# Attention scores one head at a time over four PSUM banks, with other bank partners, a later switch of order in the last tiles, and a query projection moved at the first tile

## The chip, the cores and the metric

The kernel runs on one core of one Trainium2 chip. Its time is device microseconds of that core, from the first to the last instruction of one launch. The engines are TensorE (PE, with its weight loads as PEld), VectorE (DVE), ScalarE (ACT), GpSimd (POOL) and SyncE (SP), which issues most transfers.

## What is computed

One block of cross attention and one of a routed feed-forward, both with a residual, on x of 32 batches, 256 positions and 512 features:

```python
def _mha(Q, K, V, Wq, Wk, Wv, Wo, padding_mask, attention_mask):
    n, s, e = Q.shape
    q = (Q @ Wq.T).reshape(n, s, NUM_HEADS, HEAD_DIM).transpose(0, 2, 1, 3)
    k = (K @ Wk.T).reshape(n, s, NUM_HEADS, HEAD_DIM).transpose(0, 2, 1, 3)
    v = (V @ Wv.T).reshape(n, s, NUM_HEADS, HEAD_DIM).transpose(0, 2, 1, 3)
    scores = jnp.einsum('nhqd,nhkd->nhqk', q, k) / math.sqrt(HEAD_DIM)
    scores = jnp.where(pm, scores, neg_inf)
    scores = jnp.where(attention_mask[:, None, :, :], scores, neg_inf)
    attn = jax.nn.softmax(scores, axis=-1)
    attn = jnp.where(jnp.isnan(attn), 0.0, attn)
    out = jnp.einsum('nhqk,nhkd->nhqd', attn, v)
    return out.transpose(0, 2, 1, 3).reshape(n, s, e) @ Wo.T
...
x = x + _mha(_layernorm(x), ctx, ctx, Wq, Wk, Wv, Wo, pad, mask)
x = x + ffn(_layernorm(x))      # one of 8 experts for each position, the same in all batches
```

There are 16 heads of 32 features. Of the 256 keys only the last 64 are not masked in these inputs; the kernel finds that on the chip and takes a short path (`SHORT`), which handles one block of 64 keys (`BK`).

## The kernel before

**Tiling.** The attention works on 64 tiles of 128 queries. Four tiles (two batches) form a group g; q = t mod 4 is a tile's place in its group. For each group PE projects keys (K), transposes them (KT), projects values (V) and queries in four quarters m = 0 to 3 (Q), each a block of twelve matmuls with 512 columns: every product of F32 data is made as three products of rounded high and low parts (`three`). The experts' part follows the attention and isn't touched.

**The four blocks of a tile on PE**, in this order for most tiles (`tiles` in `short_tensor`):
- `transpose_p(t)` (L1609): eight transposes of the normalised weights of tile t into PSUM tensor `pT`; ACT copies them to `pt` in two halves (`pt_copy`, semaphore `p_copied`).
- `project_o(t - 1)`: the output product of the tile before, twelve matmuls.
- `scores(t + 2)` (L1598): the scores of two tiles on. A matmul handles two heads: 64 rows of the query quarter (two heads' features), 128 query columns as weights, and 128 moving columns of `kd`, in which the two heads' keys stand on a diagonal with zeros beside them. Eight such matmuls write 1024 scores a query into `pS[:, 0]`, two banks.
- `weigh_v(t)` (L1622): 16 matmuls of 64 keys by 32 feature columns as weights and 128 queries moving, into `pA`.

After them come the projections of the next groups: two Q blocks where q is 0, one Q where it is 1, V and K where it is 2, KT and a Q where it is 3.

**PSUM.** Eight banks: `pS[:, 0]` (two) for scores, `pS[:, 1]` (two) in turn for all projections and outputs (`bank_of`, `free_bank`, `fills`), `pT` (two), `pA` (two).

**Softmax.** DVE reads the scores from PSUM. For most tiles `bias_scores` adds the mask's bias (L1349, which frees the scores' banks, semaphore `s_drained`) and `shift_biased` finds the maximum and subtracts (L1356, L1360). For the tiles in `pe_masks` (0, 1 and the last five) PE adds the bias itself, with two matmuls of an identity (L1593) ahead of the scores, and `shift_scores` reads PSUM twice (L1330, L1332). ACT makes the exponentials (L1212), DVE sums them (L1366), POOL multiplies by the inverse (`normalise_p`, L1111, semaphore `p_ready`), and PE transposes.

**Order.** Each engine's program is written out by hand. `scores_late(t)` holds for t < 57: scores(t + 2) stands behind project_o(t - 1). `scores_first(t)` holds for t = 57 to 61: scores(t + 2) stands straight behind transpose_p(t), and ACT takes the exponentials earlier in its order. ACT's order in a tile is: copies of the transposes, rounding of new inputs, `ot_high` (L1222, reads `pA`), copies of projections, exponentials of tile t + 2, and y_normalise (L1228) of tile t - 2.

**Keys.** `kt_copy` (ACT) takes the transposed keys from PSUM to `kd` in eight pieces of 32 partitions. `kd` is zeroed once at the start by DVE and POOL (`zeroed`).

The lines around the scores:

```python
for m in range(KC):
    for g2 in range(2):
        half = slice(g2 * 64, (g2 + 1) * 64)
        mm = pe.matmul(pS[:, 0, g2 * 512 + m * P:g2 * 512 + (m + 1) * P],
                       h.qt[half, g % 2, m, q * P:(q + 1) * P], h.kd[half, g % 2, q // 2, m, :],
```

## Time and profile before

| what | value |
|---|---|
| median of 3 runs | 871.42 us (871.19 to 871.42) |
| the profiled execution | 871.33 us, its span 869.5 us |
| PE busy | 97% of the span |
| DVE busy | 80% |
| POOL busy | 72% |
| ACT busy | 50% |

The span runs from the first to the last instruction; 1.8 us of the execution's time lie around it. A PE that is busy all the time isn't at its peak, since matmuls overlap and their ends are modelled; their starts are recorded.
### The profile page before, as it was taken

To read this page: it belongs to the slowest core of one execution; us is meant where nothing else is said; L and a number is where in the kernel's file an instruction comes from. 1 tells how busy PE (TensorE), PEld (TensorE's weight loads), DVE (VectorE), ACT (ScalarE), POOL (GpSimd) and SP (SyncE) were. 2 spreads that over 40 slices of the span, in tenths; PEclk is the share of its full clock that TensorE was granted. 3 is DMA by queue.
4 is the path that set the end of the run, shared out by engine and by line. 5 is a ranking of instruction groups with operands and counts; after the bars stand their busy time and mean duration, and the time that the engine had idled before them with its cause. 6 is when DMAs were issued, how large, how long until landed. Compare 5 with 4: busy or idle time off the path is not lost. (4 is left out here: it accounts for less than half of the span.)

```text
span 869.5 us, 19093 instructions
## 1 busy us (share of the span) xinstructions
PE 843.0 (97%) x6509; PEld 676.7 (78%) x6510; DVE 697.8 (80%) x1021; ACT 434.9 (50%) x762; POOL 630.0 (72%) x826
## 2 busy tenths in 40 slices
PE   8999999999999999999999999999993999999996
PEld 6778887778878888778877888777762788888885
DVE  5988888788888888788888888788778877777774
ACT  5655556565755556555756556555465222222221
POOL 3798778686768668686768668685675677777774
PEclk9999999999999999999999999999996999999998
DMA  9613342524252442524243442522488899999993
GB/s 341 226 43 92 116 136 74 171 74 136 74 157 88 135 135 74 170 77 136 74 154 95 132 133 76 162 83 77 141 270 283 256 282 293 291 281 290 286 293 110
DMA packets 123130, 141.70 MB, mean 163 GB/s; under 512 B 16128, under 2 KB 89376, under 8 KB 120992
## 3 DMA queue, kind: packets, MB, share of 16 engines
q1 hardware_dynamic: 108656, 99.45, 36.5%
q0 software_dynamic: 11360, 35.66, 12.8%
q10 hardware_dynamic: 3024, 5.45, 2.2%
q8 instruction: 49, 0.80, 0.4%
q14 instruction: 41, 0.34, 0.1%
HBM read 90.18 MB, written 51.90 MB: 163 GB/s over the span
## 5 line engine op out<-in xcount | busy, mean ns | idle before, releaser
L1827 PE MATMUL pA<-wf_hl,x_hi 128*128 x560 | 139.2, 391 | 1.8 <-DVE wf_hl L356 1.1
L1827 PEld LDWEIGHTS pA<-wf_hl,x_hi 128*128 128x128 f32 x560 | 105.4, 189 | 24.3 <-issue 2.6
L1111 POOL TENSOR_TENSOR s<-s,row 128x1024 f32<-128x1024 f32 x64 | 121.8, 1903 | 3.1 <-DVE row L1371 3.1
L1768 ACT CAST x_hi<-x2t 128x512 fp32r<-128x512 f32 x70 | 43.5, 621 | 147.1 <-PE pA L1827 136.4
L1519 PE MATMUL pS<-wo_hi,ot_hi 128*128 128x512 f32 x256 | 106.9, 418 | 0.3 <-DVE ot_lo L1375 0.3
L1087 POOL TENSOR_SCALAR y_mom<-y_mom 128x1 f32<-128x1 f32 x64 | 15.9, 248 | 124.9 <-DVE y_mom L1392 123.8
L1519 PE MATMUL pS<-xt_hi,wq_hi 128*128 128x512 f32 x256 | 105.3, 411 | 0.2 <-DVE wq_lo L1412 0.2
L1222 ACT CAST ot_hi<-pA 128x512 fp32r<-128x512 f32 x64 | 37.6, 587 | 128.9 <-PE pA L1622 128.8
L1519 PE MATMUL pS<-wo_lo,ot_hi 128*128 128x512 f32 x256 | 100.9, 394 | 0.0
L1519 PE MATMUL pS<-wo_hi,ot_lo 128*128 128x512 f32 x256 | 100.8, 394 | 0.0
L1519 PE MATMUL pS<-xt_lo,wq_hi 128*128 128x512 f32 x256 | 100.6, 393 | 0.0
L1745 POOL DMA_INDIRECT yg<-y_scratch,gather_rows x70 | 80.1, 1144 | 28.0 <-issue 27.7
L1519 PE MATMUL pS<-xt_hi,wq_lo 128*128 128x512 f32 x256 | 100.2, 391 | 0.0
L1071 POOL TENSOR_TENSOR xt_lo<-xt_raw,xt_hi 128x512 fp32r<-128x512 f32 x64 | 94.4, 1507 | 6.0 <-ACT xt_hi L1179 6.0
L1751 POOL DMA_INDIRECT out_dram<-y,scatter_rows x70 | 72.0, 1029 | 28.1 <-issue 19.8
L1349 DVE TENSOR_TENSOR s<-pS,bias 128x1024 f32<-128x1024 f32 x57 | 69.7, 1223 | 27.8 <-PE pS L1598 27.7
L1791 DVE TENSOR_TENSOR y<-pA,yg 128x512 f32<-128x512 f32 x70 | 48.4, 691 | 48.2 <-PE pA L1827 48.2
L1366 DVE TENSOR_REDUCE row<-s 128x16 f32<-128x1024 f32 x64 | 76.9, 1202 | 11.3 <-ACT s L1212 11.3
L1206 ACT COPY qt<-pS 128x512 f32<-128x512 f32 x64 | 37.6, 587 | 87.0 <-PE pS L1519 87.0
L1598 PEld LDWEIGHTS pS<-kd,qt 64*128 64x128 f32 x1024 | 62.1, 187 | 23.3 <-issue 23.3
L1212 ACT ACTIVATE s<-s,rstd 128x1024 f32<-128x1024 f32 x64 | 73.8, 1153 | 10.1 <-DVE s L1360 9.7
L1360 DVE SCALAR_TENSOR_TENSOR s<-row,s 128x1024 f32<-128x1024 f32 x57 | 76.7, 1346 | 2.0
(134 smaller groups left out, 1937.6 us busy)
## 6 DMA issues: line engine op xcount, KB each, us to landing
xq<-x_scratch SPq DMA_DIRECT2D x280, 64.0 KB
xt_raw<-in_x_t SPq DMA_DIRECT2D x16, 1024.0 KB, 6.9
x<-in_x SPq DMA_DIRECT2D x64, 256.0 KB, 3.2
y_scratch<-y_biased SPq DMA_DIRECT2D x64, 256.0 KB, 2.1
x_scratch<-y_normal SPq DMA_DIRECT2D x64, 256.0 KB, 2.9
wf_hl<-in_wf ACTq DMA_DIRECT2D x5, 1024.0 KB, 6.1
ctx_raw<-in_ctx_t SPq DMA_DIRECT2D x32, 128.0 KB, 3.0
wf_hl<-in_wf SPq DMA_DIRECT2D x3, 1024.0 KB, 8.7
```

The lines of the kernel that those rows point to most:

```text
L1071: pool.tensor_tensor(h.xt_lo[:, k, :], h.xt_raw[:, k, :], h.xt_hi[:, k, :].bitcast(F32), ALU.subtract)\
L1111: pool.tensor_tensor(p, p, h.row[:, t % h.c, 3, :].unsqueeze(2).broadcast_to([P, H, BK]), ALU.mult)\
L1212: act.activation(p, p, ACT.Exp, scale=h.rstd[:, t % h.c, 2:3]).then_inc(exp_ready, 1)
L1349: dve.tensor_tensor(h.s_sb[:, t % h.c, :].rearrange("p (h k) -> p h k", h=H), pS[:, 0, :].rearrange("p (h k) -> p h k", h=H), h.bias[:, t ...
L1360: dve.scalar_tensor_tensor(p, h.row[:, t % h.c, 0, :].unsqueeze(2).broadcast_to([P, H, BK]), FLOOR, p, ALU.max, ALU.subtract).then_inc(shi ...
L1366: dve.tensor_reduce(row[:, 1, :], h.s_sb[:, t % h.c, :].rearrange("p (h k) -> p h k", h=H), AX.X, ALU.add).then_inc(sum_ready, 1)
L1519: mm = pe.matmul(dst, lhs[a], rhs[b], start=(k == 0 and n == 0), stop=(k == KC - 1 and n == 2))
L1598: mm = pe.matmul(pS[:, 0, g2 * 512 + m * P:g2 * 512 + (m + 1) * P], h.qt[half, g % 2, m, q * P:(q + 1) * P], h.kd[half, g % 2, q // 2, m, ...
L1745: pool.indirect_dma_start(yg[:, r, :], None, y_rows, bass.IndirectOffsetOnAxis(ap=gather_rows[:, j:j + 1], axis=0))\
L1751: pool.indirect_dma_start(out, bass.IndirectOffsetOnAxis(ap=scatter_rows[:, j:j + 1], axis=0), y2[:, j % 3, :], None, bounds_check=last_ro ...
L1791: dve.tensor_tensor(y2[:, j % 3, :], pA[:, j % 2, :], yg[:, j % R, :], ALU.add).then_inc(y2_ready, 1)
L1827: return pe.matmul(pA[:, r % 2, :], rows[:, r % 2, c * P:(c + 1) * P], w, start=first, stop=last)
```

## The change

It has four parts.

**Scores.** A matmul now handles one head: 32 rows of features, 64 queries as weights, 64 keys moving. There are 4 (m) x 2 (halves of the queries) x 4 (j, the 32-row quarters) = 32 of them for a tile. Quarter j writes bank 2 + j, 256 columns of it (`pF`). `kd` loses its zeros and half its size, one ACT copy fills it, and the two memsets with their waits are gone. DVE reads and writes the same 1024 elements in patterns with four banks. The heads' order on the host follows. Bias on PE is four matmuls of 256 columns in place of two of 512.

**Banks.** All eight are one tensor `banks`. Projections and outputs take banks 0 and 1, scores 2 to 5, transposes 4 and 5 as before, `pA` 6 and 7. So scores and transposes share two banks: scores(t) waits for `p_copied` of tile t - 2, and transpose_p(t) waits until the scores of tile t + 1 are drained.

**Order in the last tiles.** `scores_first` holds for t = 59 to 61 and `scores_late` for t < 59; PE adds the bias for the last three tiles only. ACT's order follows.

**Tile 0.** project_q(1, 1) stands ahead of scores(2).

```diff
-        self.pe_masks = (0, 1) + tuple(range(self.tiles - 5, self.tiles))
+        self.pe_masks = (0, 1) + tuple(range(self.tiles - 3, self.tiles))
...
     def scores_late(self, t):
-        return t < self.tiles - 7
+        return t < self.tiles - 5
 
     def scores_first(self, t):
-        return self.tiles - 7 <= t < self.tiles - 2
+        return self.tiles - 5 <= t < self.tiles - 2
...
-        pS = top.enter_context(nc.psum_tensor("pS", [P, 2, 2 * 512], F32))
-        pT = top.enter_context(nc.psum_tensor("pT", [P, 2, 512], F32))
-        pA = top.enter_context(nc.psum_tensor("pA", [P, 2, 512], F32))
+        banks = top.enter_context(nc.psum_tensor("banks", [P, 8, 512], F32))
+        pS = banks[:, 0:4, :].rearrange("p (r b) n -> p r (b n)", r=2)
+        pT = banks[:, 4:6, :]
+        pA = banks[:, 6:8, :]
+        pF = banks[:, 2:6, 0:HG * BK].rearrange("p j (m k) -> p j m k", m=KC)
...
             def kt_copy(g):
-                if g == 0:
-                    act.wait_ge(zeroed, 2)
                 act.wait_ge(kt_done, g + 1)
-                for j in range(HG):
-                    r = slice(j * DH, (j + 1) * DH)
-                    src = bank("KT", g)[r, :].rearrange("p (c s k) -> p c s k", c=KC, s=2)
-                    for s in range(2):
-                        ins = act.copy(h.kd[r, g % 2, s, :, (j % 2) * BK:(j % 2 + 1) * BK], src[:, :, s, :])
-                ins.then_inc(kt_copied, 1)
+                act.copy(h.kd[:, g % 2], bank("KT", g).rearrange("p (c s k) -> p s c k", c=KC, s=2)).then_inc(kt_copied, 1)
...
             def scores(t):
                 g, q = divmod(t, h.c)
                 wait(pe, s_drained, t)
+                wait(pe, p_copied, 2 * (t - 1))
...
-                    for g2 in range(2):
-                        pe.matmul(pS[:, 0, g2 * 512:(g2 + 1) * 512].rearrange("p (h k) -> p h k", h=H // 2), ident_r[:],
-                                  h.bias[:, r:r + 1, :].broadcast_to([P, H // 2, BK]), start=True, stop=False)
+                    for j in range(HG):
+                        pe.matmul(pF[:, j], ident_r[:], h.bias[:, r:r + 1, :].broadcast_to([P, KC, BK]), start=True, stop=False)
                 for m in range(KC):
-                    for g2 in range(2):
-                        half = slice(g2 * 64, (g2 + 1) * 64)
-                        mm = pe.matmul(pS[:, 0, g2 * 512 + m * P:g2 * 512 + (m + 1) * P],
-                                       h.qt[half, g % 2, m, q * P:(q + 1) * P], h.kd[half, g % 2, q // 2, m, :],
-                                       start=not biased, stop=not biased or m == KC - 1)
+                    for half in range(2):
+                        rows = slice(half * 64, (half + 1) * 64)
+                        for j in range(HG):
+                            dims = slice(j * DH, (j + 1) * DH)
+                            mm = pe.matmul(pF[rows, j, m, :], h.qt[dims, g % 2, m, q * P + half * 64:q * P + (half + 1) * 64],
+                                           h.kd[dims, g % 2, q // 2, m, :], start=not biased, stop=not biased or m == KC - 1)
                 mm.then_inc(s_done, 1)
 
             def transpose_p(t):
                 pe.wait_ge(p_ready, t + 1)
+                pe.wait_ge(s_drained, min(t + 2, h.tiles))
...
                     if t > 0:
                         project_o(t - 1)
+                    if t == 0:
+                        project_q(g + 1, 1)
                     if h.scores_late(t):
                         scores(t + 2)
                     weigh_v(t)
...
+                    if q == 0 and 0 < t and g + 1 < h.groups:
+                        project_q(g + 1, 1)
                     if q == 0 and g + 1 < h.groups:
-                        project_q(g + 1, 1)
                         project_q(g + 1, 2)
```

PE's instructions at tile 0, before: transposes of tile 0, then straight the scores of tile 2, weights times values, and the Q blocks.

```order
L1609 MATMUL pT<-ident,s 128x128 [waits p_ready]
L1609 MATMUL pT<-ident,s 128x128 x7
L1598 MATMUL pS<-kd,qt 128x128 [waits s_drained]
L1598 MATMUL pS<-kd,qt 128x128 x7
L1622 MATMUL pA<-pt,vd 32x128 [waits p_copied,v_copied]
```

After, of the same place (all PSUM is called `banks`; the Q block has twelve matmuls):

```order
L1604 MATMUL banks<-ident,s 128x128 [waits s_drained,p_ready]
L1604 MATMUL banks<-ident,s 128x128 x7
L1512 MATMUL banks<-xt_hi,wq_hi 128x512 [waits kt_copied,xt_lo_ready]
...
L1593 MATMUL banks<-kd,qt 64x64 [waits p_copied,s_drained]
L1593 MATMUL banks<-kd,qt 64x64 x31
L1617 MATMUL banks<-pt,vd 32x128 [waits p_copied,v_copied]
```

A Q block stands between transposes and scores now, the scores are 32 matmuls, and they wait for the copies of the transposes.

PE's instructions at tile 60, before: transposes of tile 60, bias and scores of tile 62, the output product of tile 59.

```order
L1609 MATMUL pT<-ident,s 128x128 [waits p_copied,p_ready]
L1609 MATMUL pT<-ident,s 128x128 x3
L1609 MATMUL pT<-ident,s 128x128 [waits p_copied]
L1609 MATMUL pT<-ident,s 128x128 x3
L1593 MATMUL pS<-bias,ident_r 128x512 [waits bias_ready,ident_rounded,s_drained]
L1593 MATMUL pS<-bias,ident_r 128x512
L1598 MATMUL pS<-kd,qt 128x128 x8
L1519 MATMUL pS<-wo_hi,ot_hi 128x512 [waits ot_lo_ready,v_copied]
```

After, at tile 60:

```order
L1604 MATMUL banks<-ident,s 128x128 [waits p_copied,s_drained,p_ready]
L1604 MATMUL banks<-ident,s 128x128 x3
L1604 MATMUL banks<-ident,s 128x128 [waits p_copied]
L1604 MATMUL banks<-ident,s 128x128 x3
L1587 MATMUL banks<-bias,ident_r 128x256 [waits ident_rounded,bias_ready,p_copied,s_drained]
L1587 MATMUL banks<-bias,ident_r 128x256 x3
L1593 MATMUL banks<-kd,qt 64x64 x32
L1512 MATMUL banks<-wo_hi,ot_hi 128x512 [waits ot_lo_ready,v_copied]
```

The order of the blocks is the same, but the bias now waits for `p_copied` of the transposes just ahead, and the transposes for `s_drained`. In tiles 57 and 58 the output product stands ahead of the scores in the new order, as in all tiles before them.

## Rows read from the trace of the kernel before

**Rows 1.** The page's first part: busy us (share of the span) and instructions.

```profile
PE 843.0 (97%) x6509; PEld 676.7 (78%) x6510; DVE 697.8 (80%) x1021; ACT 434.9 (50%) x762; POOL 630.0 (72%) x826
```

**Rows 2.** PE's waits: who waited for whom, total us, times, longest.

```profile
PE pT L1609 <- POOL s L1111: 1.4, 2, 0.8
```

**Rows 3.** Timeline of tile 27: start us, us from first start to last end.

```profile
305.73 1.03 PE L1609 MATMUL pT<-ident,s 128*128 128x128 f32 x8
306.52 0.48 PE L1519 MATMUL pS<-wo_hi,ot_hi 128*128 128x512 f32 x1
...
309.49 1.16 PE L1598 MATMUL pS<-kd,qt 64*128 64x128 f32 x16
310.58 0.67 PE L1622 MATMUL pA<-pt,vd 64*32 64x128 f32 x32
310.80 1.23 DVE L1349 TENSOR_TENSOR s<-pS,bias 128x1024 f32<-128x1024 f32 x1 [0.51 <-PE pS L1598]
311.18 0.65 PE L1558 MATMUL pS<-ident,k 128*128 128x128 f32 x4
311.35 0.59 ACT L1222 CAST ot_hi<-pA 128x512 fp32r<-128x512 f32 x1 [3.16 <-PE pA L1622]
```

**Rows 4.** Timeline, two windows that end up to 0.14 us after V's first start.

```profile
310.58 0.34 PE L1622 MATMUL pA<-pt,vd 64*32 64x128 f32 x8
...
310.58 0.40 PE L1622 MATMUL pA<-pt,vd 64*32 64x128 f32 x9
```

**Rows 5.** Loads and matmuls by line (ns min/median/max), an F32 block, its mean ns.

```profile
L1598 PEld LDWEIGHTS pS<-kd,qt x1024: 182/188/188, 31.3 to 633.3; 64*128 64x128 f32 x171
...
L1622 PEld LDWEIGHTS pA<-pt,vd x2048: 102/107/107, 44.9 to 647.3; 64*32 64x32 f32 x187
L1622 PE MATMUL pA<-pt,vd x2048: 269/269/294, 44.9 to 647.4; 64*32 64x128 f32 x187
...
11.83 3.60 PE L1648 MATMUL pT<-wq_raw,ones 128*128 128x512 f32 x8
...
L1648 PE MATMUL pT<-wq_raw,ones 128*128 128x512 f32 x8 | 3.6, 592 | 0.0
```

**Rows 6.** Timeline, scores of tile 7, then ACT and the scores of tile 8.

```profile
94.08 0.60 PE L1598 MATMUL pS<-kd,qt 64*128 64x128 f32 x6
...
99.67 1.15 ACT L1212 ACTIVATE s<-s,rstd 128x1024 f32<-128x1024 f32 x1 [0.23 <-DVE s L1360]
100.73 0.80 ACT L1228 ACTIVATE y_normal<-y 128x512 f32<-128x512 f32 x1
101.44 1.05 ACT L1217 COPY pt<-pT 128x512 f32<-128x512 f32 x2
...
102.42 1.16 PE L1598 MATMUL pS<-kd,qt 64*128 64x128 f32 x16
```

**Rows 7.** Timeline at the start: POOL's normalise of tile 2, PE's first transposes of it.

```profile
57.44 1.91 POOL L1111 TENSOR_TENSOR s<-s,row 128x1024 f32<-128x1024 f32 x1
...
59.45 0.40 PE L1609 MATMUL pT<-ident,s 128*128 128x128 f32 x2
```

**Rows 8.** Timeline of the last tiles: T(57), bias, S(61), T(62), V(63), DVE's experts.

```profile
599.91 1.03 PE L1609 MATMUL pT<-ident,s 128*128 128x128 f32 x8
...
618.80 0.71 PE L1593 MATMUL pS<-bias,ident_r 128*128 128x512 f32 x2
619.45 1.16 PE L1598 MATMUL pS<-kd,qt 64*128 64x128 f32 x16
...
637.39 1.09 PE L1609 MATMUL pT<-ident,s 128*128 128x128 f32 x8
...
647.05 0.67 PE L1622 MATMUL pA<-pt,vd 64*32 64x128 f32 x32
...
655.63 12.20 DVE L356 TENSOR_TENSOR wf_hl<-wf_hl 128x2048 fp32r<-128x2048 f32 x5 [1.34 <-POOL y L1091]
```

**Rows 9.** Line view: the moments of an input tile on DVE, mean ns of one.

```profile
L1321 DVE BATCH_NORM_STATS2 stat<-x 128x6 f32<-128x512 f32 x64 | 42.4, 662 | 0.6 <-DVE s L1332 0.6
```

More of the change, by code:

```diff
@@ L275, in kernel_program @@
         h.k_sb = sb("k", [P, DM], F32, st)
-        h.kd = sb("kd", [P, 2, h.nb, KC, 2 * BK], F32, st)
+        h.kd = sb("kd", [P, 2, h.nb, KC, BK], F32, st)
+        sb("rest_of_kd", [P, 2 * h.nb * KC * BK], F32, st)
         h.qt = sb("qt", [P, 2, KC, h.c * P], F32, st)
@@ L911, in scores @@
                             half = slice(g2 * 64, (g2 + 1) * 64)
-                            mm = pe.matmul(pS[:, ring, g2 * 512 + m * P:g2 * 512 + (m + 1) * P],
-                                           f.qt[half, m, q * P:(q + 1) * P],
+                            pair = pS[:, ring, g2 * 512:(g2 + 1) * 512].rearrange("p (e m k) -> p m e k", e=2, m=KC)
+                            mm = pe.matmul(pair[:, m], f.qt[half, m, q * P:(q + 1) * P],
                                            f.kd[half, (q // 2) * f.nbk + n, m, :], start=True, stop=True)
@@ L1115, in short_gpsimd @@
             pool.memset(neg_half[:], -0.5).then_inc(ones_set, 1)
-            pool.memset(h.kd[:, 1], 0.0).then_inc(zeroed, 1)
             ctx_low(0)
@@ L1328, in shift_scores @@
                 dve.wait_ge(s_done, t + 1)
-                s = pS[:, 0, :].rearrange("p (h k) -> p h k", h=H)
-                dve.tensor_reduce(h.row[:, t % h.c, 0, :], s, AX.X, ALU.max).then_inc(max_ready, 1)
+                top_of = h.row[:, t % h.c, 0, :].rearrange("p (j m) -> p j m", j=HG)
+                dve.tensor_reduce(top_of, pF, AX.X, ALU.max).then_inc(max_ready, 1)
                 dve.wait_ge(max_ready, t + 1)
-                dve.scalar_tensor_tensor(h.s_sb[:, t % h.c, :].rearrange("p (h k) -> p h k", h=H),
-                                         h.row[:, t % h.c, 0, :].unsqueeze(2).broadcast_to([P, H, BK]), FLOOR, s,
+                dve.scalar_tensor_tensor(h.s_sb[:, t % h.c, :].rearrange("p (j m k) -> p j m k", j=HG, m=KC),
+                                         top_of.unsqueeze(3).broadcast_to([P, HG, KC, BK]), FLOOR, pF,
                                          ALU.max, ALU.subtract).then_inc(shifted, 1)
@@ L1348, in bias_scores @@
                 dve.wait_ge(s_done, t + 1)
-                dve.tensor_tensor(h.s_sb[:, t % h.c, :].rearrange("p (h k) -> p h k", h=H),
-                                  pS[:, 0, :].rearrange("p (h k) -> p h k", h=H),
-                                  h.bias[:, t % (2 * h.c):t % (2 * h.c) + 1, :].bitcast(F32).broadcast_to([P, H, BK]), ALU.add)\
+                dve.tensor_tensor(h.s_sb[:, t % h.c, :].rearrange("p (j m k) -> p j m k", j=HG, m=KC), pF,
+                                  h.bias[:, t % (2 * h.c):t % (2 * h.c) + 1, :].bitcast(F32).unsqueeze(1)
+                                  .broadcast_to([P, HG, KC, BK]), ALU.add)\
                     .then_inc(s_drained, 1)
@@ L1383, in residual @@
                 b = h.bank_of("O", t)
-                dve.tensor_tensor(y_sb[:, t % 2, 0:DM], pS[:, 1, b * 512:(b + 1) * 512], h.x_sb[:, t % (2 * h.c), :], ALU.add)\
+                dve.tensor_tensor(y_sb[:, t % 2, 0:DM], pS[:, 0, b * 512:(b + 1) * 512], h.x_sb[:, t % (2 * h.c), :], ALU.add)\
                     .then_inc(added, 1)
@@ L1419, in halves_wide @@
                 return a.unsqueeze(2).broadcast_to([P, 2, n])
-            dve.memset(h.kd[:, 0], 0.0).then_inc(zeroed, 1)
             for c in range(2):
@@ L1474, in short_vector @@
             dve.wait_ge(rp, 3)
-            done(dve.tensor_scalar(rows_f[:, 0, :], pT[:, 1, NR:2 * NR], c_batch, None, ALU.add))
-            done(dve.tensor_scalar(rows_f[:, 1, :], pT[:, 1, 0:NR], -float(OOB), float(OOB), ALU.mult, ALU.add))
+            done(dve.tensor_scalar(rows_f[:, 0, :], pA[:, 0, 264 + NR:264 + 2 * NR], c_batch, None, ALU.add))
+            done(dve.tensor_scalar(rows_f[:, 1, :], pA[:, 0, 264:264 + NR], -float(OOB), float(OOB), ALU.mult, ALU.add))
             done(dve.tensor_copy(gather_rows[:], rows_f[:, 0, :]))
@@ L1664, in short_tensor @@
                 n, i = divmod(k, PB)
-                mm = pe.matmul(pT[:, 1, 0:2 * NR].rearrange("p (a n) -> p a n", a=2), place[:, i * P:(i + 1) * P].bitcast(BF16),
+                mm = pe.matmul(pA[:, 0, 264:264 + 2 * NR].rearrange("p (a n) -> p a n", a=2), place[:, i * P:(i + 1) * P].bitcast(BF16),
                                match[:, n, :, i * NR:(i + 1) * NR], start=(k == 0), stop=(k == 2 * PB - 1))
@@ L1960 @@
     pad = a["mask_BxS2_bf1"].reshape(B, 2, P).transpose(2, 0, 1)
-    head_order = [g2 * H // 2 + 2 * m + e for m in range(KC) for g2 in range(2) for e in range(2)]
+    head_order = [KC * j + m for m in range(KC) for j in range(HG)]
     rows = np.concatenate([np.arange(h * DH, (h + 1) * DH) for h in head_order])
```

6 lines of the change are left out of this document (2 added, 4 removed).

## The prediction

> Below, T(t), S(t), O(t) and V(t) are TensorE's four blocks of query tile t: transposing its weights, its scores, its output product, and weights times values. P is any block of twelve 512-column projections.
>
> **What bounds the kernel now.** I read the page's busy shares first: PE is busy in 97% of the span [rows 1]. PE's list of waits then shows that it stood for others in hardly anything but the seam to the experts: the attention part's only entry is 1.4 us for POOL [rows 2]. So in tiles 2 to 58 time is what PE's blocks take from start to start. The timeline of one tile gives them: T and O together 3.76 us (305.73 to 309.49), S 1.09 us (to 310.58), V 0.60 us (to 311.18) [rows 3]. Four tiles with four Q blocks, two more for K and V, and four O make 39.2 us a group. The change rewrites S, so the question is what 64 small matmul passes take where 16 larger ones took 1.09 us, and who is late once PE is faster.
>
> **The scores block.** Every F32 matmul shows as two records, each with a weight load. S has 8 matmuls of 64 rows by 128 columns, so 16 records; the new S has 32 of 32 rows by 64 weight columns and 64 keys, so 64 records. S's 16 take 1.16 us with the tail of the last, 0.27, so it starts at 0.89 and they stand 59 ns apart on average [rows 3]. Narrow windows show that in V eight start together, 7 ns apart (one lasts at most 0.294, 8 end at 0.34), and the ninth starts at 0.40 - 0.27 = 0.13 us [rows 4, 5]. So independent parts of the array work side by side: eight in V (two row halves, four column quarters), and two in S (two row halves). V's 32 records are four waves of eight; the last record starts at 0.67 - 0.27 = 0.40, so a wave is 0.11 us. In S eight waves of two fit the same: seven of them in 0.89 us, the first longer by its load.
>
> What is a wave's length? An F32 stream of 512 columns takes (3.60 - 0.59)/7 = 0.43 us, so 0.84 ns a column: 107 ns for the 128 columns of S and V, 54 ns for 64 keys [rows 5]. Loads: 188 ns for 128 weight columns, 107 for 32, so 0.84 ns a column again: 54 ns for 64 [rows 5]. In S load (107) and stream (107) overlap, as waves come every 0.11 us. In the new S four row quarters by two column halves are again eight parts; each matmul of one m sits in a part of its own and row quarter j writes its own bank. A wave is the longest of load 54, stream 54 and eight issues of 6.8 = 54 ns; I take 57, with the 3 ns that the other waves have over 107. The first wave waits for its load, so the second starts at 106 ns; six more take 342; the last record starts 48 later, at 496 ns. From the last start to the next block it was 1.09 - 0.89 = 0.20 us with a stream of 107; with 54 it is 0.146. **S is then 0.64 us, 0.45 less.** I exclude less than 0.60: eight streams and a drain are 0.58 alone. Upwards, the nearest rows are V's mean of 0.40/31 = 12.9 ns a record, which would be 63 x 12.9 + 146 = 0.96 us, if it were the rate at which PE takes in long runs: V's 32 pairs follow S's 16, and never have 64 pairs come in a row. I take 0.64, since V's waves of eight show 7 ns inside and a gap of their stream's length after.
>
> Against this change speaks a rule. The rows show starts 7 ns apart [rows 4]. The Trainium skill, "TensorE: Matmul & The Clock Gate", section "Wait — 56ns, not 53.3ns?", says that matmuls never start closer than about 25 ns apart, however small; this trace disagrees within a wave, and with V's mean of 12.9. By that rule S would be an estimated 64 x 25 + 146 ns, 1.75 us.
>
> **How many of the 64 count.** At the start POOL sets the time: its normalise ends at 59.35, and T(2) starts at 59.45 [rows 7], with the DMA issues and mask work before it on POOL untouched. So what S(0) to S(3) save (S(3) comes before T(2)) is waited away. S(4) to S(58) count: 55 x 0.45 = **-24.8 us**. At tile 0 the Q block moved ahead of S(2) covers the wait for the copies.
>
> **New waits in the steady part.** Scores now share two banks with the transposes. S(t+2) waits until ACT has copied T(t). With O between them there are 3.76 us, and the tightest tile of a group (the third) has copies from 101.44 to 102.49 while S starts at 102.42 [rows 6]: already 0.07 too late. ACT is late there because copies stand behind exp and normalise of the chain that began with the scores one tile earlier. Chain and next S both move 0.45 earlier, so the miss stays 0.07, with 0.04 for the signal (an estimate): 0.11 x 14 groups = **+1.5 us** (bounds 0 and 0.3 each, 4 us). T(t+1) also waits until DVE has drained S(t+2). V and at least one P (3.4 us) lie between, DVE starts to read 1.3 us after S and takes 1.2 [rows 3]; this costs nothing before tile 59. Behind both waits stand the following blocks of PE, all in order.
>
> **The last tiles.** From tile 59 no P is left. There S(t+2) stands ahead of O(t), so nothing covers the wait for copies; before it waited for no copies. From T(57) at 0: tiles 57 and 58 are 3.76 + 0.64 + 0.60 + 2.8 (a P, taken as O's 2.97 less the split's change) = 7.8 us each, so T(59) is at 15.7 and S(60) was at 11.7. The chain from an S to the end of ACT's copies for the tile before takes 8.4 us (94.08 to 102.49) [rows 6], now 8.0; tile 57 also has two pairs of moments on DVE, 0.66 us each and their aggregates [rows 9], of which I let 1.1 be late. Copies of T(59) end at 20.8, and PE, done with T(59) at 16.5, stands for 4.3 us. Then bias matmuls 0.65 (the same columns as before, 618.80 to 619.45 [rows 8]), S 0.64, O 2.97 (306.52 to 309.49, with the change of array split [rows 3]), V 0.60: T(60) at 25.7. For the next two, the copies end 0.77 (V to ot_high [rows 3]) + 0.49 + 1.06 + 0.71 + 1.05 (exp, normalise, copies [rows 6]) = 4.1 us after V's start, so T(61) is at 34.1, T(62) at 42.5. From T(62) to V(63) the order stays: 9.66 us [rows 8], plus 0.2 for ACT work pushed together. V(63) is at 52.4 where it was at 647.05 - 599.91 = 47.1 [rows 8]: **+5.2 us**, all savings there included (bounds +2.5, if DVE isn't late and normalise finds room elsewhere, and +7). What follows V(63) hangs on DVE from 655.63 on [rows 8] and moves with it.
>
> ACT copies keys once, not in eight pieces, and DVE and POOL drop a memset. PE waits for ACT nowhere in its list before the experts [rows 2], so there is nothing to gain; if ACT had stood between, it would show there. DVE reads the same 1024 elements from four banks: nothing; ten per cent more would add 0.1 us to the chain and so 1.7 us in all. DVE biases tiles 59 and 60 in place of PE: contained above.
>
> **Sum.** -24.8 + 1.5 + 5.2 = -18.1 on the profiled execution's 871.33 us (the median of the runs is 871.42): **853.3 us**.
>
> **The rivals.**
> 1. *Copies of the tail hidden, or shorter waves* (0.05): tail +2 and S 0.61, so 847 to 849.
> 2. *PE takes in long runs no faster than V's mean* (0.13): S 0.96, so -0.13 x 55 = -7.2, the tail +5.2 + 5 x 0.32 = +6.8, waits +1.5: 872.4, no change. For it: no run of 64 pairs in the trace. Against: eight records within 50 ns.
> 3. *Slower: two column halves of one row quarter load one after the other* (0.12). Load is 107 ns a wave, waves of 111, S = 160 + 6 x 111 + 50 + 146 = 1.02 us: -0.07 x 55 = -3.9, tail +5.2 + 5 x 0.38 = +7.1, waits +1.5: 876. As 55 + 5 blocks carry S, the total is 8.95 - 60 x (1.09 - S), which ends slower by 0.2% once S is over 0.97 us. For it: in V four column quarters of 32 add to 107 ns too, as long as its waves. Against: V's ninth record comes at 0.13 us, and its second wave would not be finished starting at 0.18 had the fourth quarter's first load ended at 0.11 and streamed 0.107 more.
> 4. *A floor of 25 ns per record* (0.06): S 1.75, so +0.66 x 55 = +36, the tail +8.5, no stall at the copies: 916. The skill's rule above would act so; the mechanism is PE's issue, and V speaks against it.
> The forecast, with S between 0.60 and 0.80 and the tail within its bounds, has 0.64 and reaches from 848.5 to 863.
>
> The range 848.5 to 873 takes in the forecast and rival 2. A measurement can tell about 0.2%, 1.7 us. Faster by more: 0.64 + 0.05 and a little of rival 2, 0.70; same 0.11; slower 0.19.
>
> **What would show it.** Right: 64 records of S with its last start near 0.5 us, a group of four tiles near 37.5 us, PE idle about 4 us before S(61) and 3 us before S(62) and S(63), POOL the releaser of T(1) and T(2). Wrong in the block: waves of 0.11 us, or steady starts 13 or 25 ns apart. Wrong in the waits: an idle PE before S or T in every tile, or copies of tiles 59 to 61 that end before T does plus 1.5 us.

## The result and the profile after

The changed kernel takes **876.29 us** (median of five runs, 874.5 to 878.9), the kernel before 871.42 beside it (871.11 to 871.92): a ratio of 1.0053, 95% interval 1.0038 to 1.0068. It is slower by half a per cent, where I had predicted 853.3 and a range up to 873.0. The profiled execution took 875.45 us, its span 873.7, so 4.1 us more than that of before.

The page's first part, to be read against [rows 1]: PE is busy 10.8 us less, with half as many instructions again, and the span is longer all the same. POOL is where it was, DVE has 4.4 us more and ACT 29.9 less.

```profile
PE 832.2 (95%) x9587; PEld 669.3 (77%) x9588; DVE 702.2 (80%) x1022; ACT 405.0 (46%) x650; POOL 630.0 (72%) x825
...
q8 instruction: 73, 1.20, 0.5%
```

PE's list of waits (who waited for whom, total us, times, longest), where the tiles of the kernel before had 1.4 us for POOL [rows 2] and 0.3 for `ot_lo`; its start waited 1.6 us for the first weights, which my reading of that list as a single entry had left out. "issue" names no engine. L1587 is now the bias, L1593 S, L1512 a projection or O, L1604 T:

```profile
PE banks L1587 <- issue: 8.7, 3, 3.7
PE banks L1512 <- issue: 2.4, 1, 2.4
PE banks L1512 <- DVE wk_lo L1406: 2.4, 1, 2.4
...
PE banks L1593 <- ACT pt L1211: 0.8, 2, 0.6
PE banks L1604 <- POOL s L1113: 0.8, 1, 0.8
```

The timeline of a steady tile (start us, us from first start to last end), as [rows 3]:

```profile
302.88 1.03 PE L1604 MATMUL banks<-ident,s 128*128 128x128 f32 x8
306.64 0.91 PE L1593 MATMUL banks<-kd,qt 32*64 32x64 f32 x64
307.49 0.67 PE L1617 MATMUL banks<-pt,vd 64*32 64x128 f32 x32
```

T and O still take 3.76 us in three of the four tiles of a group, and S leads V by 0.85 us (0.84 by the records' own nanoseconds) in place of 1.09. The saving is 0.25 us, not 0.45.

The path divides at two tiles: T(2), to which POOL releases PE [rows 7], and T(57). T's starts in the two timelines:

| stretch | before | after | difference | predicted |
|---|---|---|---|---|
| start to T(2) | 59.45 | 61.10 | +1.7 | 0 |
| T(2) to T(57) | 540.5 | 532.2 | -8.2 | -23.3 |
| T(57) to T(63) | 43.3 | 54.0 | +10.7 | +5.2 (to V(63)) |
| T(63) to the end of the execution | 228.1 | 228.1 | 0 | 0 |

Three places show where the time went. First the last tiles, the timeline from T(59), PE and the ACT copies of T(59); rows of O between are left out:

```profile
609.63 1.03 PE L1604 MATMUL banks<-ident,s 128*128 128x128 f32 x8
613.23 1.07 ACT L1211 COPY pt<-banks 128x512 f32<-128x512 f32 x2
614.41 0.71 PE L1587 MATMUL banks<-bias,ident_r 128*128 128x256 f32 x4 [3.74 <-issue]
615.05 1.11 PE L1593 MATMUL banks<-kd,qt 32*64 32x64 f32 x64
616.09 0.80 PE L1512 MATMUL banks<-wo_hi,ot_hi 128*128 128x512 f32 x1
...
617.11 0.63 PE L1512 MATMUL banks<-wo_hi,ot_lo 128*128 128x512 f32 x1
617.53 0.63 PE L1512 MATMUL banks<-wo_hi,ot_hi 128*128 128x512 f32 x1
...
619.36 0.39 PE L1512 MATMUL banks<-wo_hi,ot_lo 128*128 128x512 f32 x1
619.59 0.40 PE L1512 MATMUL banks<-wo_hi,ot_hi 128*128 128x512 f32 x1
...
620.38 0.67 PE L1617 MATMUL banks<-pt,vd 64*32 64x128 f32 x32
620.98 1.09 PE L1604 MATMUL banks<-ident,s 128*128 128x128 f32 x8
```

PE stands 3.74 us for the copies of T(59), as foreseen (4.3). The view gives no releaser ("issue"), but ACT's copies end at 614.30 and the bias starts at 614.41. But then O's first matmuls come 0.43 us apart and its last 0.23: the granted clock falls to the 1.2 GHz level at 615.6, 1.2 us after PE has started again, and stays there until 619.0, and O takes 4.29 us instead of 2.97. The same follows the 2.48 us before S(62) and S(63), which start behind ACT's copies too. The windows view of the same ten microseconds (PE, PEld, DVE, ACT and POOL busy, PEclk, DMA share, GB/s) gives the granted clock at 0.83; in the kernel before it is 1.00 there:

```profile
620.00:630.00 10.00, 7.52 (x121) 5.74 (x121) 6.18 (x9) 3.30 (x5) 5.15 (x8) 0.83 0.52 159
```

Second, a stop in the middle of a Q block of tile 32, where PE waits for no engine; the timeline of PE, its loads, SP's queue:

```profile
354.35 0.47 SPq L992 DMA_DIRECT2D xt_raw<-in_x_t  x1
...
354.86 0.50 PE L1512 MATMUL banks<-xt_hi,wq_hi 128*128 128x512 f32 x1
...
357.73 0.39 PE L1512 MATMUL banks<-xt_lo,wq_hi 128*128 128x512 f32 x1 [2.38 <-issue]
357.73 0.19 PEld L1512 LDWEIGHTS banks<-xt_hi,wq_lo 128*128 128x128 f32 x1 [2.58 <-issue]
```

Third, the start: the first K block waits 2.35 us for the first weights (1.41 before), and nine of its twelve matmuls then come at the lower clock level:

```profile
7.76 0.56 PE L1512 MATMUL banks<-wk_hi,ctx_hi 128*128 128x512 f32 x1 [2.35 <-DVE wk_lo L1406]
8.12 0.63 PE L1512 MATMUL banks<-wk_lo,ctx_hi 128*128 128x512 f32 x1
...
11.48 0.40 PE L1512 MATMUL banks<-wk_hi,ctx_hi 128*128 128x512 f32 x1
```

### The profile page after: what moved, and what is told of

Its sections match the earlier page's. It is cut to its first block and busy times, and to the rows that moved or that the text cites. A ratio compares the mean times of both kernels' runs of the same rounds, so it can differ in the third digit from the quotient of the medians.

```text
span 873.7 us, 25195 instructions
## 1 busy us (share of the span) xinstructions
PE 832.2 (95%) x9587; PEld 669.3 (77%) x9588; DVE 702.2 (80%) x1022; ACT 405.0 (46%) x650; POOL 630.0 (72%) x825
## 5 line engine op out<-in xcount | busy, mean ns | idle before, releaser
L1825 PE MATMUL banks<-wf_hl,x_hi 128*128 x560 | 138.8, 390 | 2.3 <-ACT x_hi L1766 1.2
L1825 PEld LDWEIGHTS banks<-wf_hl,x_hi 128*128 128x128 f32 x560 | 105.0, 188 | 24.7 <-issue 3.1
L1512 PE MATMUL banks<-wo_hi,ot_hi 128*128 128x512 f32 x256 | 108.9, 425 | 0.5 <-DVE ot_lo L1369 0.5
L1512 PE MATMUL banks<-xt_hi,wq_hi 128*128 128x512 f32 x256 | 105.2, 411 | 0.2 <-DVE wq_lo L1406 0.2
L1512 PE MATMUL banks<-wo_lo,ot_hi 128*128 128x512 f32 x256 | 102.3, 400 | 0.0
L1512 PE MATMUL banks<-wo_hi,ot_lo 128*128 128x512 f32 x256 | 102.2, 399 | 0.0
L1512 PE MATMUL banks<-xt_lo,wq_hi 128*128 128x512 f32 x256 | 99.8, 390 | 2.4 <-issue 2.4
L1512 PE MATMUL banks<-xt_hi,wq_lo 128*128 128x512 f32 x256 | 100.5, 393 | 0.1
L1343 DVE TENSOR_TENSOR s<-banks,bias 128x1024 f32<-128x1024 f32 x59 | 72.2, 1224 | 17.2 <-PE banks L1593 17.0
L1098 POOL TENSOR_TENSOR y_biased<-y,bias_at 128x512 f32<-128x512 f32 x64 | 76.4, 1193 | 0.0
```

What stands on the lines that cost most here:

```text
L1098: pool.tensor_tensor(y_biased[:, t % Y_RING, :], y_sb[:, t % 2, 0:DM], bias_at[:, t % 2, :], ALU.add)\
L1343: dve.tensor_tensor(h.s_sb[:, t % h.c, :].rearrange("p (j m k) -> p j m k", j=HG, m=KC), pF, h.bias[:, t % (2 * h.c):t % (2 * h.c) + 1, :] ...
L1512: mm = pe.matmul(dst, lhs[a], rhs[b], start=(k == 0 and n == 0), stop=(k == KC - 1 and n == 2))
L1825: return pe.matmul(pA[:, r % 2, :], rows[:, r % 2, c * P:(c + 1) * P], w, start=first, stop=last)
```

## The experiments

The theory after the result: the shared banks make S wait for the copies, in the last tiles without cover; PE's clock then falls; and S is 0.84 us since only some of its records start in the waves I had counted. The kernel before was run beside each group, 871.6 to 872.3 us. All edits are to the changed kernel unless said. "Steady" is T(0) to T(57), "tail" T(57) to T(63), both from the timelines of the profiled executions.

| run | steady | tail | median us | ratio to before (95%) |
|---|---|---|---|---|
| before | 557.0 | 43.3 | 871.42 | 1 |
| after | 548.7 | 54.0 | 876.29 | 1.0053 (1.0038 to 1.0068) |
| late_tail | 548.6 | 48.0 | 868.92 | 0.9957 (0.9942 to 0.9973) |
| old_switch | 548.5 | 57.5 | 879.34 | 1.0080 (1.0058 to 1.0102) |
| old_scores | 559.6 | 55.0 | 887.06 | 1.0169 (1.0148 to 1.0190) |
| only_switch | 557.1 | 42.8 | 871.55 | 1.0001 (0.9992 to 1.0010) |
| fill_tail | 550.5 | 49.7 | 870.71 | 0.9979 (0.9964 to 0.9994) |
| copies_first_late | 550.1 | 48.5 | 868.97 | 0.9958 (0.9941 to 0.9975) |
| copies_first | 548.7 | 50.0 | 871.06 | 0.9986 (0.9973 to 0.9998) |
| pe_shift | 552.0 | 48.0 | 875.29 | 1.0031 (1.0017 to 1.0045) |
| share_a | 543.0 | 46.2 | 859.81 | 0.9865 (0.9850 to 0.9880) |
| share_a_59 | 543.0 | 47.3 | 861.09 | 0.9874 (0.9858 to 0.9889) |

### Waits and clock in the last tiles

**late_tail.**

```diff
-        self.pe_masks = (0, 1) + tuple(range(self.tiles - 3, self.tiles))
+        self.pe_masks = (0, 1)
...
     def scores_late(self, t):
-        return t < self.tiles - 5
+        return t < self.tiles - 2
 
     def scores_first(self, t):
-        return self.tiles - 5 <= t < self.tiles - 2
+        return False
```

> The changed kernel, but the last tiles keep the order of all others: scores(t+2) stands behind project_o(t-1) up to tile 61, DVE adds the bias in all of them. Theory (the tail loses its time in the uncovered wait for ACT's copies ahead of S(61) to S(63), and in PE's lower clock after that idle time): O covers the wait, PE never idles over 2 us, the granted clock stays at its full level, and tiles 59 to 62 come every 7.5 to 8.2 us in place of 11.4, 10.2, 10.2 and 6.1. T(57) to T(63) falls from 54.0 to about 47 us and the whole to 869 us. Rival (the chain from scores to transposes, two tiles long, sets the end, and S standing later makes it longer): T waits for POOL in place of S for ACT, periods of 9.5 us or more, 874 to 880 us.

Measured: 868.92 us, tail 48.0 us, so the order that never switches is 7.4 us better than the change's. In the timeline the waits are split between ACT ahead of S and POOL ahead of T:

```profile
620.79 0.90 PE L1593 MATMUL banks<-kd,qt 32*64 32x64 f32 x64 [2.07 <-ACT pt L1211]
...
623.19 1.09 PE L1604 MATMUL banks<-ident,s 128*128 128x128 f32 x8 [0.90 <-POOL s L1113]
```

The theory's total came, though not its claims that O would cover the wait (2.07 us are left, and 2.01 in the next tile) and that the clock would stay. Behind the 2.07 us it stays; behind the 2.01 us it falls, and O in tile 62 takes 4.86 us. The windows view, columns as above, gives 1.00 from 622 to 630 us and then:

```profile
630.00:637.00 7.00, 6.12 (x49) 5.05 (x50) 6.38 (x8) 3.17 (x5) 3.52 (x5) 0.53 0.56 159
```

**fill_tail.**

```diff
                     if h.scores_first(t):
+                        keep_clock(pe, 12, banks[:, 2, :], w_hi["o"][:, 0, 0:P], w_hi["o"][:, 0, :])
                         scores(t + 2)
```

> The changed kernel with twelve matmuls of 512 columns (about 2.8 us of useless work into a free bank) between T(t) and S(t+2) in tiles 59 to 61, which keep PE busy while it would wait for ACT's copies. Theory (part of the tail's loss is PE's clock, which falls to the 1.2 GHz level after the idle time, so that O's first matmuls stand 0.43 us apart in place of 0.23): the granted clock stays 1.00 from 609 to 640 us, each of the three tiles is 1.3 us shorter, 872 us. Rival (the chain through ACT, DVE and POOL sets the tiles' period and PE's clock is hidden under it): periods unchanged at 10.2 us, 876 us, or more if the filler overshoots the wait.

Measured: 870.71 us (866.5 to 873.0), tail 49.7 us, 4.3 less than the changed kernel, for work that computes nothing. Timeline and windows:

```profile
620.22 3.01 PE L1506 MATMUL banks<-wo_hi 128*128 128x512 f32 x12
623.07 0.64 PE L1587 MATMUL banks<-bias,ident_r 128*128 128x256 f32 x4
623.64 0.91 PE L1593 MATMUL banks<-kd,qt 32*64 32x64 f32 x64
624.48 0.50 PE L1512 MATMUL banks<-wo_hi,ot_hi 128*128 128x512 f32 x1
```

```profile
620.00:630.00 10.00, 10.00 (x142) 8.04 (x141) 7.30 (x11) 4.59 (x8) 5.16 (x8) 1.00 0.49 159
```

S starts at the same distance from T as before (4.2 us, 4.3 with the filler), O is back at 2.97 us, and a tile takes 8.7 us instead of 10.15. So the clock is worth 1.4 us in each of the three tiles, and it was on the path.

**old_switch.** The last tiles' numbers as in the kernel before.

```diff
-        self.pe_masks = (0, 1) + tuple(range(self.tiles - 3, self.tiles))
+        self.pe_masks = (0, 1) + tuple(range(self.tiles - 5, self.tiles))
...
-        return t < self.tiles - 5
+        return t < self.tiles - 7
...
-        return self.tiles - 5 <= t < self.tiles - 2
+        return self.tiles - 7 <= t < self.tiles - 2
```

> The changed kernel with the order of the last tiles as before: scores ahead of the output product from tile 57 on, bias on PE for the last five tiles. Theory (each such tile has an uncovered wait for the copies of its own transposes of 2 to 4 us): two more tiles wait, so 3 us each on top, less what the chain gains: 879 to 882 us. Rival (the earlier switch brings scores forward, and the wait is the same however early): 873 to 876 us.

Measured: 879.34 us. Tiles 57 and 58 take 10.5 us each instead of 8.1 and 8.2: a wait of 1.52 us is uncovered there too. So with these banks the later switch was better than the earlier one, and no switch at all (late_tail) better than both.

**old_scores and only_switch** put the parts apart from the other side, on the kernel before. old_scores has every part but the new block; only_switch has, of that, neither of the two waits:

```diff
             def scores(t):
                 g, q = divmod(t, h.c)
                 wait(pe, s_drained, t)
+                wait(pe, p_copied, 2 * (t - 1))
...
             def transpose_p(t):
                 pe.wait_ge(p_ready, t + 1)
+                pe.wait_ge(s_drained, min(t + 2, h.tiles))
```

> The kernel before with everything of the change but the new block of scores and its banks: the two waits (scores for the copies two tiles back, transposes for drained scores), the later switch, bias on PE for the last three, the query projection ahead of S(2). So S stays at 1.09 us and 16 records. Theory (sharing banks costs 1.5 to 3 us in the steady tiles and the tail's waits about 11 us; the new block gives 0.25 us x 55 = 13.8 us back): 883 to 886 us, with the tail T(57) to T(63) near 54 us. Rival (the tail's loss comes from the new block's many instructions and not from the wait): 873 to 876 us. If the late start of T(0) (+1.8 us) and the stop of 2.4 us for instructions belong to the changed block's 3078 more PE instructions, both are absent here.

> The kernel before with the later switch (from tile 59), bias on PE for the last three tiles and the query projection ahead of S(2), nothing else: the old scores block, the old banks, no new waits. Against the run old_scores it lacks only the two waits. Theory (the waits cost the tail some 10 us and the steady tiles 2.5 us, the switch hardly anything): T(57) to T(63) 43 to 45 us, 871 to 873 us. Rival (the switch lengthens the tail): 50 us or more, 878 us or more.

Measured: 887.06 us, just over my 883 to 886, and 871.55. The two waits alone cost 15.5 us: 2.5 in the steady part, 12.2 in the tail (55.0 against 42.8), the rest at the start. The waiting times with the old block are the same to the hundredth as in the changed kernel, and the clock falls after them as well (S's row is 2.08 us long, not 1.16):

```profile
624.91 1.19 PE L1594 MATMUL pS<-bias,ident_r 128*128 128x512 f32 x2 [3.74 <-issue]
626.03 2.08 PE L1599 MATMUL pS<-kd,qt 64*128 64x128 f32 x16
...
635.26 1.19 PE L1594 MATMUL pS<-bias,ident_r 128*128 128x512 f32 x2 [2.48 <-issue]
```

The switch by itself costs nothing (0.1 us of the median). Neither run has a stop for instructions.

**copies_first_late and copies_first** try to shorten the tail's loop: ACT copies T(t) before it takes the exponentials of tile t+1 (on late_tail, and on the changed kernel; `late_exps` holds for t = 58 to 61).

```diff
                     pt_copy(t)
+                    if h.late_exps(t - 1):
+                        exps(t + 1)
...
                     if h.scores_late(t) and not h.late_exps(t):
                         exps(t + 2)
```

> The run late_tail (scores behind the output product in all tiles) with one more change of ACT's order: from tile 58 on ACT takes the exponentials of tile t+2 only behind the copies of T(t+1). Theory (in the last tiles T(t)'s copies stand behind the exponentials of tile t+1, which ties the loop copies, scores, bias, shift, exponentials of every single tile to 8.3 us): copies end 1.8 us after T, S(t+2) starts 3.8 us after T(t), and tiles 59 to 62 come every 7.0 to 7.3 us; T(57) to T(63) 44 us in place of 48.0, 865 us. Rival (DVE or POOL sets the 8.3 us, and T waits for the later exponentials): 869 us or more.

> The changed kernel (scores ahead of the output product from tile 59) with ACT's exponentials behind the copies of the next transposes from tile 58 on. Theory as for copies_first_late: copies end 1.8 us after T, so S(t+2) starts 2.5 us after T(t) with the bias ahead; PE idles 1.0 us, too short for its clock to fall, and tiles 59 to 62 come every 6.5 to 7 us: T(57) to T(63) 43 us in place of 54.0, 864 to 866 us. Rival (PE's clock or the chain through POOL decides): periods over 8 us, 870 us or more.

Measured: 868.97 and 871.06 us. The first gains nothing over late_tail, as the rival said: S does start 3.8 us after T, but then PE waits 3.2 us for POOL ahead of T, as the exponentials come later by what the copies gained.

```profile
617.72 1.09 PE L1609 MATMUL banks<-ident,s 128*128 128x128 f32 x8 [3.19 <-POOL s L1116]
621.54 0.91 PE L1598 MATMUL banks<-kd,qt 32*64 32x64 f32 x64
```

The second brings the tail from 54.0 to 50.0 us, where I expected 43; the wait ahead of the first bias is still 2.70 us and the clock falls behind it. In copies_first_late the clock stays behind the 3.19 us and falls behind the 2.66 us of the next tile. So a better order on ACT alone gains little; that the loop through all four engines is what sets the period then is my reading, which no run tested.

### The stop for instructions

**pe_shift**, on late_tail:

```diff
             keep_clock(pe, 11, pT[:, 1, 0:P], ones[:], ones[:])
+            for _ in range(128):
+                pe.wait_ge(ones_set, 1)
             project_k(0)
```

> The run late_tail with 128 waits for a semaphore that is long set, in PE's program ahead of its first K block, where PE waits for weights anyway: PE's instruction stream is shifted by about half an instruction packet and nothing else changes. Theory (the stop of 2.5 us in the middle of a Q block at T(34) + 2 us, at the same place of the program in all kernels with the new scores block, is PE waiting for its next packet of instructions, which collides with the group's bulk loads): the stop moves or goes, 866.5 us if it goes. Rival (something else at that place of the program): it stays at the same place with the same length, 869 us.

Measured: 875.29 us, over both figures that I had given. The waits themselves were not free: T(0) starts at 45.7 us, not 42.8. The stop (it is in tile 32, which starts at 349.65 us in the changed kernel, and not in T(34)) is gone, and another of 3.1 us stands behind 202 us, in a block that ran through in every other kernel, a shorter one of 0.9 us before 325.3:

```profile
201.83 0.67 PE L1617 MATMUL banks<-pt,vd 64*32 64x128 f32 x32
205.57 0.47 PE L1512 MATMUL banks<-xt_hi,wq_hi 128*128 128x512 f32 x1 [3.08 <-issue]
```

Besides the position of PE's instructions only the late start changed, and the stop had stood at the same place of the program with T(32) anywhere from 347.5 to 349.7 us; so it goes with the supply of instructions. In the changed kernel the queue for instructions moves 73 packets where before it was 49, of 16 KB each (1.20 MB in 73, 0.80 in 49), and a packet starts at 355.4 us, inside the stop and behind the group's bulk loads (SP's row above). The packets' starts in the traces say more: the median distance from one to the next is 9.0 us, but this one comes 15.4 us after its forerunner (340.0), and both stops of pe_shift stand at distances of 15.4 us too (187.6 to 203.0, 307.4 to 322.8). In share_a and share_a_59, further below, no distance before T(57) is over 12.6 us, and neither has a stop. The distance alone doesn't decide: others of 13 to 15.2 us cost nothing, or 0.4 us in tile 44. The Trainium skill, "Runtime: NRT & Kernel Launch", section "Instruction fetch mechanics", describes refills in 16 KB blocks that are mostly hidden; the packets agree, and where a stop was not hidden it took 2.3 to 3.1 us, the two short ones apart. That bulk loads are what makes one packet late was not tried. After some of these stops the clock falls too: in fill_tail (a stop of 2.32 us) and copies_first_late (2.65) the Q block after the same stop has matmuls 0.43 us apart, and the tile takes 1.6 and 1.9 us longer than in late_tail, where the clock stayed behind 2.38 us. This is most of the difference in their steady times. Whether it is also what spreads the changed kernel's runs over 4.4 us isn't shown: the kernel before spreads over 0.8 us beside it, but over 3.3 and 4.7 beside two later groups of runs.

### What the 64 records do

The timeline's windows with S's line alone (PE busy and instructions that had started), in the changed kernel, S starting at 306.64:

```profile
306.60:306.70 0.10, 0.06 (x8) 1.00 1.77 492
...
306.60:306.92 0.32, 0.28 (x32) 1.00 1.15 346
306.60:307.00 0.40, 0.36 (x34) 1.00 1.10 348
...
306.60:307.34 0.74, 0.70 (x64) 1.00 1.00 322
```

Eight start within 0.05 us, 32 by 0.28: the waves of eight are there, as predicted. Then only two more start in 0.08 us, and the last 32 need 0.42 us, 13.3 ns each.

**half_scores and three_quarters** issue only the last half, or the last three quarters, of the block in tiles 3 to 60; the edit is that of half_scores, and the other has 1 in place of 2.

```diff
-                for m in range(KC):
+                for m in range(0 if t < 3 or biased else 2, KC):
```

> The changed kernel in which only the second half of the scores' matmuls is issued (m = 2 and 3 of 0 to 3) for tiles 3 to 60: 16 matmuls, 32 records. Half of the heads' scores are left out. Theory (the first 32 or so records of a block stand queued at PE and start in waves of eight, 58 ns apart; what comes after them starts only as fast as PE takes instructions in, 16.7 ns per record with its load): the last of 32 starts at 0.27 us, V follows S by 0.42 us in place of 0.84, but V's own 32 records are then no longer queued and V takes about 0.7 us in place of 0.60; the steady group falls by 4 x 0.3 = 1.2 us and the whole to 860 us. Rival (it is m = 2 and 3 themselves that are slow, by their place in the banks): 16.7 ns apart from the start, V follows S by 0.66 us, 866 us. The stop of 2.5 us for instructions near T(34) disappears or moves, as PE's stream is shorter.

> The changed kernel in which three of four parts of the scores' matmuls are issued (m = 1 to 3) for tiles 3 to 60: 24 matmuls, 48 records. A quarter of the heads' scores are left out. Theory (when S begins some 11 records stand ready at PE, and PE takes in one more every 13.3 ns, so record n starts no earlier than (n - 11) x 13.3 ns: this fits 64 records with the last start at 0.70 and 32 with 0.27): the last of 48 starts at 0.48 to 0.50 us, V follows S by 0.63 to 0.65 us, V itself stays at 0.67. Rival A (waves of eight for all 48, and only the last 16 of 64 are slow): last start 0.39, V at 0.53 us. Rival B (the first 32 are quick and every later one stands 16.7 ns behind the one before): last start 0.54, V at 0.69 us. The whole, from 0.20 us less in each of 53 tiles, 10.6 us under the changed kernel's 876, 865 us, give or take 3 for the start and the stops for instructions.

Measured: half_scores 853.38 us (851.9 to 854.8), three_quarters 865.4 in a single run. Timelines, first of half_scores, then of three_quarters; S to V is 0.42 and 0.71 us:

```profile
306.64 0.49 PE L1593 MATMUL banks<-kd,qt 32*64 32x64 f32 x32 [0.76 <-ACT pt L1211]
307.06 0.33 PE L1617 MATMUL banks<-pt,vd 64*32 64x128 f32 x6
```

```profile
302.24 0.78 PE L1593 MATMUL banks<-kd,qt 32*64 32x64 f32 x48
302.95 0.51 PE L1617 MATMUL banks<-pt,vd 64*32 64x128 f32 x17
```

32 records are quick whichever m they are; so it isn't their place in the banks. V stays at 0.60 us from start to start, so my 860 us was too high: half the block saves the full 0.42 us of S. For 48 records the model of a stock of 11 and an intake of 13.3 ns, which had fitted 32 and 64, said 0.63 to 0.65 and falls; rival B, the first 32 quick and the others 16.7 ns apart, said 0.69, and the records stand at just these 16.7 ns from the 35th on. With 64 some twelve of the last third come faster again, 8.3 ns apart. share_a, below, has the same starts to 1 ns with other bank partners. **So it is shown that a block of such matmuls is quick for its first 32 or 33 records and then stands 8 to 17 ns a record; what limits it (how PE takes instructions in, or how many it may have open) stays open.**

### Other bank partners

**share_a**, with the numbers of the last tiles as before, and **share_a_59** with the change's. The transposes share banks 6 and 7 with V's products instead; scores keep four banks.

```diff
             def scores(t):
-                wait(pe, p_copied, 2 * (t - 1))
...
             def transpose_p(t):
                 pe.wait_ge(p_ready, t + 1)
-                pe.wait_ge(s_drained, min(t + 2, h.tiles))
+                wait(pe, ot_lo_ready, t)
...
-                        mm = pe.transpose(pT[:, b, r * P:(r + 1) * P], ...
+                        mm = pe.transpose(pA[:, b, r * P:(r + 1) * P], ...
...
             def weigh_v(t):
-                    pe.wait_ge(p_copied, 2 * t + c + 1)
+                    if c == 0:
+                        pe.wait_ge(p_copied, 2 * t + 2)
```

> The changed kernel's scores block with other bank partners: the transposes go to banks 6 and 7, where V's products stand, and the scores have banks 2 to 5 alone. So neither new wait is there; T(t) waits instead until DVE has read the products of V(t-1) (ot_low), and V(t) for both copies of T(t). Order of the last tiles and bias on PE as in the kernel before (from tile 57, last five). Theory (the new block itself is worth 0.25 us x 54 = 13.4 us less the 2.6 us stop for instructions, and all that the change lost in the tail and 2.5 us in the steady tiles came from scores and transposes sharing banks): T(0) to T(57) 546 us against 557.0 and 548.6, T(57) to T(63) 42 to 43 us against 43.3 and 54.0, 860 us. Rival (the new wait only moves: T(t) stands for ot_low in each tile, 0.2 to 0.5 us, and in the last tiles 1 to 2 us): 870 to 880 us.

> The run share_a, but with the change's later switch (scores ahead of the output product from tile 59, bias on PE for the last three). Theory (the later switch by itself costs little, since the waits behind it are gone; but S(61) comes 2 us later for the chain of T(61)): T(57) to T(63) 43 to 45 us, 860 to 862 us. Rival (the later switch is itself what lengthens the tail): 48 us or more, 866 us.

Measured: 859.81 us (859.3 to 860.3) and 861.09: **share_a is 1.35% faster than the kernel before, the best of all that leave nothing out.** share_a_59 differs from the changed kernel in the partners and their waits alone: 861.09 against 876.29. In share_a PE's list of waits has nothing in the steady tiles, and no stop for instructions; two of its entries:

```profile
PE banks L1603 <- issue: 6.1, 4, 1.5
PE banks L1512 <- DVE wk_lo L1406: 1.8, 2, 1.6
```

From T(2) to T(57) it is 14.4 us less than before, 0.26 in each of 55 tiles. V already waited for the copies of T(t), and O for `ot_low`, so for most tiles the new partners share a wait that stood there anyway. In the tail the new wait is 1.5 us a tile, until DVE's `ot_lo` ends at 618.05, and the granted clock is 1.00 from 605 to 625 us all the same; the tail is 46.2 us against 43.3, where I expected 42 to 43. In share_a_59 it is 47.3 (expected 43 to 45): there the first wait is 2.76 us and the clock falls.

```profile
617.36 0.69 DVE L1369 TENSOR_TENSOR ot_lo<-banks,ot_hi 128x512 fp32r<-128x512 f32 x1 [0.59 <-ACT ot_hi L1216]
618.15 1.06 PE L1603 MATMUL banks<-ident,s 128*128 128x128 f32 x8 [1.51 <-issue]
...
619.61 0.91 PE L1592 MATMUL banks<-kd,qt 32*64 32x64 f32 x64
```

## Why the prediction was wrong

The forecast was 18.1 us under the profiled execution of before; it came 4.1 over. Half of the 22 us between is one step, the saving of S at 0.45 us a tile, which measured 0.25; a quarter is the last tiles, where the lower clock had no price. By its own terms:

| term | predicted | measured | missed by |
|---|---|---|---|
| S's saving, 55 tiles | 0.45 each, -24.8 | 0.25 each, -13.8 | 11.0 |
| waits in the steady part | +1.5 | +2.6 | 1.1 |
| stops for instructions (tile 32, tile 44) | not foreseen | +2.5 and +0.4 | 2.9 |
| the last tiles | +5.2 | +10.7 | 5.5 |
| the start | 0 | +1.7 | 1.7 |

**The scores block.** Right: the waves of eight, 58 ns long, the second at 107 ns, and the tail of 0.146 us (0.147). Wrong: the step that carried them on to 64 records. I had noted that "V's 32 pairs follow S's 16, and never have 64 pairs come in a row", put V's mean of 12.9 ns into a rival as a rate for the whole block, and left the case between unpriced. The truth is the mixture: 32 records by the waves, 0.28 us, then 32 at 13.3 ns, 0.42 us, 0.84 with the tail, outside the 0.60 to 0.80 that the forecast allowed. Rival 2 had the rate for half the block, but not its 0.96 us. Rival 3 falls with its waves of 111 ns: they are 58. Rival 4, a floor of 25 ns between starts, falls with 32 starts in 0.28 us.

**How many count, and the start.** That S(0) to S(3) save nothing held: T(2) comes 8.35 us after T(1), as before. But the whole start was 1.7 us later, which isn't the change's: T(0) starts between 42.4 and 45.3 us in kernels with the same start, and 44.4 in share_a_59 against 42.4 in share_a, with the first K block at 8.0 and 6.9 us. It goes with how early the first weights land and which clock the K block then gets. A single profile carries this as if it were a term; how much of it the medians carry isn't on record.

**New waits.** The third tile of a group misses by 0.19 us, not 0.11 (T to S is 3.95 us), and some early tiles by 0.2 to 0.6. From T to S that is 3.8 us over all tiles; 1.2 come back, as V to the next T is 0.02 to 0.05 us shorter. old_scores confirms the sum at 2.5 us. That the wait for drained scores costs nothing in the steady tiles was right.

**The last tiles.** The mechanism was right: the wait for copies uncovered, idle PE of 3.74 us (predicted 4.3) and twice 2.48. What it set off was missed: the granted clock falls, and O and S of the same tile run slower, 1.4 us in each of three tiles; fill_tail gets back 4.3 us in all. The other 1.2 us are for the most part S, at 0.84 instead of 0.64 in five tiles. PE's longest wait in the tiles of the kernel before was 0.8 us [rows 2], with the clock at its upper level throughout, so no row there priced a longer one. I took O at the upper level all the same; an upper bound had to take it at the lower one, and mine of +7 did not.

**Against the rivals.** The result has the sign of rival 3 and its size, but not its cause. What decides the sign is not S's length: at 0.84 us the block is worth 14 us, as share_a shows, and the two waits that came with its banks take 15.5.

## What to carry to other kernels

When a faster block needs more banks, price the partner it must share with, not only the block: choose a partner whose release the sharer already waits for (here V's products for the transposes), and the same block turns a loss of 0.5% into a gain of 1.26% with nothing else altered (1.35% with the old order of the last tiles). Where a wait is left uncovered, ask what PE's clock does behind it. In the changed kernel it fell after 2.48 and 3.74 us, each tile lost 1.4 us more, and useless matmuls into a free bank bought that back. The length of one wait doesn't tell by itself: the clock stayed after 1.5, 2.07 and once 3.19 us, and fell after 2.01, 2.66, 2.70 and 2.76. A rate read from a short burst holds for the length of that burst.

## What the runs showed of the hardware

- Small F32 matmuls on separate parts of the array start 7 ns apart within a wave, and waves of eight follow at 58 ns, for the first 32 or 33 records of a block only; after that 16.7 ns, and for some twelve records late in a block of 64, 8.3 ns.
- PE can stop for 2.3 to 3.1 us where a packet of its instructions comes 15 us after the one before, in place of the usual 9 (not at every such distance): with some 9600 PE instructions one such stop in most kernels, at the same place of the program, another place with the stream shifted, none in share_a and share_a_59, none with 6509. Sometimes the clock falls behind it, for 1.6 to 1.9 us more.
- The granted clock fell after idle times of 2.01 to 3.74 us in the last tiles, but not after all of them (2.07 and 3.19 us), so the length of one idle time didn't decide it.
- 128 waits for a semaphore that is long set cost PE some 2.3 us at the start (first K block at 9.05 us in place of 6.7, with DVE's `wk_lo` done at 6.6 in both).
